# Routed experts in 71 tiles of 256 rows instead of 39 of 512

## The reference

```python
def _ffn(x, w1, w2, w3):
    return jax.nn.silu(x @ w1.T) * (x @ w3.T) @ w2.T
logits = xf @ router_w.T + expert_bias
rw, sel = jax.lax.top_k(logits, 2)
rw = jax.nn.softmax(rw)
combine = jnp.einsum('tk,tke->te', rw, jax.nn.one_hot(sel, 8))
# over the experts e: acc + combine[:, e, None] * _ffn(xf, w1[e], w2[e], w3[e])
```

## Time and profile before

| | us |
|---|---|
| median of three runs | 2825.15 |
| the profiled execution | 2823.8 |
| its span, on which all rows below lie | 2821.8 |
| the block of the routed experts, first row request to first request of the scan (789.61 to 1032.56) | 242.95 |

### The profile page before, as it was taken

One profiled execution on the slowest core, in us unless ns is written; L12 is line 12 of the kernel. 1 busy time (PEld: TensorE's weight loads), 2 busy tenths in 40 slices (PEclk: granted clock), 3 DMA queues, 4 the chain that ended last, 5 costly groups with the idle time before them and its releaser, 6 DMA issues. The chain is left out here.

```text
span 2821.8 us, 43246 instructions
## 1 busy us (share of the span) xinstructions
PE 2466.5 (87%) x13043; PEld 1468.7 (52%) x13058; DVE 2264.4 (80%) x3693; ACT 1704.3 (60%) x3383; POOL 2041.8 (72%) x1817
## 2 busy tenths in 40 slices
PE   7979999899979976989889898898999999995555
PEld 5646666566646642333333333333368888773222
DVE  5879999766634459999999999999867777777887
ACT  7847777743323235776667766676555555554665
POOL 5539999757746647999999999999546666664554
PEclk9979999999989987999999999999999999997555
DMA  5921111011145545545455454455523333320000
GB/s 170 422 60 22 23 23 23 7 33 44 42 130 165 153 124 183 189 172 197 171 186 186 175 193 172 186 185 203 182 83 91 88 86 88 87 81 19 19 19 23
DMA packets 238421, 331.80 MB, mean 118 GB/s; under 512 B 46433, under 2 KB 186998, under 8 KB 217346
## 3 DMA queue, kind: packets, MB, share of 16 engines
q1 hardware_dynamic: 227538, 311.48, 33.2%
q0 software_dynamic: 9088, 16.94, 1.7%
q10 hardware_dynamic: 1584, 0.79, 0.1%
HBM read 231.45 MB, written 99.50 MB: 117 GB/s over the span
## 5 line engine op out<-in xcount | busy, mean ns | idle before, releaser
L1870 POOL TENSOR_TENSOR s_drive<-s_du,s_b_sb 128x1024 f32<-128x1024 f32 x256 | 600.3, 2358 | 37.0 <-DVE s_state_ps L2237 36.8
L2237 DVE TENSOR_TENSOR_SCAN s_state_ps<-s_decay_ps,s_drive 128x512 f32<-128x512 f32 x416 | 487.1, 1216 | 42.8 <-ACT s_decay_ps L2023 33.5
L2385 PE MATMUL s_y_ps<-s_read,w_ident 128*128 128x512 f32 x832 | 406.7, 615 | 89.1 <-DVE s_read L2250 88.8
L2023 ACT ACTIVATE s_decay_ps<-s_delta,neg_rate 128x508 f32<-128x508 f32 x512 | 340.9, 682 | 152.0 <-DVE s_state_ps L2237 94.6
L2385 PEld LDWEIGHTS s_y_ps<-s_read,w_ident 128*128 128x128 f32 x832 | 149.3, 192 | 322.3 <-DVE s_read L2250 183.9
L2250 DVE TENSOR_TENSOR s_read<-s_state_ps,s_c_sb 128x1024 f32<-128x1024 f32 x208 | 254.7, 1224 | 7.2
L1416 POOL DMA_INDIRECT m_y_scratch<-e_y,e_index x156 | 152.5, 978 | 91.0 <-DVE e_y L1462 49.1
L2676 POOL TENSOR_TENSOR c_share<-c_p,c_norm 128x1232 f32<-128x1232 f32 x64 | 148.3, 2317 | 83.2 <-DVE c_norm L2809 83.2
L741 ACT ACTIVATE b_pT<-b_turn_ps 77x512 f32<-77x512 f32 x256 | 144.3, 591 | 74.6 <-PE b_turn_ps L873 74.6
L2879 PE MATMUL c_f_ps<-c_ctxT,w_c_wqk 128*128 128x308 f32 x512 | 178.4, 437 | 7.1 <-ACT c_k L2723 3.6
L1044 POOL DMA_INDIRECT m_rows_scratch<-m_xs,m_index x128 | 128.5, 1004 | 60.1 <-issue 39.9
(11 more groups left out here) (373 smaller groups left out, 6193.0 us busy)
## 6 DMA issues: line engine op xcount, KB each, us to landing
s_b_sb<-s_bc_scratch SPq DMA_DIRECT2D x64, 1024.0 KB, 6.2
s_c_sb<-s_bc_scratch SPq DMA_DIRECT2D x64, 1024.0 KB, 5.4
c_vp_scratch<-s_stage SPq DMA_DIRECT2D x152, 256.0 KB, 2.6
c_vp<-c_vp_scratch SPq DMA_DIRECT2D x64, 576.0 KB, 4.1
m_rows_scratch<-fill SPq DMA_DIRECT2D x33, 1040.0 KB, 27.0
e_w<-in_m_we_dram SPq DMA_DIRECT2D x39, 384.0 KB, 3.2
e_xg<-m_rows_scratch SPq DMA_DIRECT2D x39, 260.0 KB, 3.4
s_read<-m_y_scratch SPq DMA_DIRECT2D x32, 256.0 KB, 3.1
```

Source lines behind the costliest of these rows:

```text
L1870: nc.gpsimd.tensor_tensor(drive[:, (g * states + n) % drives, :, :], du[:, s, :, :], b_sb[:, n, :].unsqueeze(1).broadcast_to([128, halves, ...
L2023: nc.scalar.activation(decay[:, m, :, 1:], delta[:, s, m, :].rearrange("p (b t) -> p b t", t=T)[:, :, 1:], ACT.Exp, scale=core.neg_rate[:, ...
L2237: nc.vector.tensor_tensor_scan(home[:, h, :], decay[:, h, :, :].rearrange("p b t -> p (b t)"), drive[:, (g * states + n) % drives, h, :], ...
L2385: last = nc.tensor.matmul(y_ps[:, m, :], core.ident[:, :], read[:, r % deep, m, :], start=False, stop=False)
```

## The change

The tile of the routed experts gets a size of its own, `ET` = 256 rows; `TILES` becomes 2 * 8192 / 256 + 7 = 71. Both halves of the hidden units of a tile lie side by side in one PSUM bank (2 x 256 columns), so gate, value, result and transposed rows have two banks each, used in turn, and silu and the product run once for a tile, over 512 columns. PE's order becomes up(t), turn_x(t+2), down(t-1). SP first asks for the rows of four tiles, and then in turn for the weights of tile t and the rows of tile t+4. Rows and results have eight slots, weights five. The table is 71 entries wide.

```diff
+ET = 256
-LONGEST = B * T // GT
-TILES = 2 * B * T // GT + 7
+LONGEST = B * T // ET
+TILES = 2 * B * T // ET + 7
...
-    halves = 2
-    x_slots, w_slots, y_slots = 5, 3, 5
+    halves, lots = 2, ET // 128
+    x_slots, w_slots, y_slots, ahead = 8, 5, 8, 4
...
-        g_ps = ps("e_g_ps", [128, halves, GT])
-        u_ps = ps("e_u_ps", [128, halves, GT])
-        o_ps = ps("e_o_ps", [128, 2, GT])
-        turn_ps = ps("e_turn_ps", [128, GT])
+        g_ps = ps("e_g_ps", [128, 2, halves * ET])
+        u_ps = ps("e_u_ps", [128, 2, halves * ET])
+        o_ps = ps("e_o_ps", [128, 2, 512])
+        turn_ps = ps("e_turn_ps", [128, 2, 512])
...
-            for t in range(TILES):
+            def load_x(t):
                 first = sp.value_load(table[0][0:1, t:t + 1], min_val=0, max_val=8 * REGION)
-                owner = sp.value_load(table[1][0:1, t:t + 1], min_val=0, max_val=7)
                 if t >= x_slots:
                     sp.wait_ge(x_turned.sem, x_turned.at(t - x_slots, 1))
                     sp.wait_ge(y_ready.sem, y_ready.at(t - x_slots, 1))
                     sp.wait_ge(x_in[t % x_slots].sem, x_in[t % x_slots].at(t // x_slots, 0))
...
+            def load_w(t):
+                owner = sp.value_load(table[1][0:1, t:t + 1], min_val=0, max_val=7)
                 if t >= w_slots:
                     sp.wait_ge(downed.sem, downed.at(t - w_slots, 1))
...
+            for t in range(ahead):
+                load_x(t)
+            for t in range(TILES):
+                load_w(t)
+                if t + ahead < TILES:
+                    load_x(t + ahead)
...
             copy_xT(0)
+            copy_xT(1)
             for t in range(TILES):
-                if t + 1 < TILES:
-                    copy_xT(t + 1)
-                for n in range(halves):
-                    open_gate(t, n)
+                open_gate(t)
+                if t + 2 < TILES:
+                    copy_xT(t + 2)
...
-            def up(t, n):
+            def up(t):
                 pe.wait_ge(xT_ready.sem, xT_ready.at(t, 1))
                 landed(pe, w_in, t)
-                if t >= 1:
-                    pe.wait_ge(h_ready.sem, h_ready.at(t - 1, n + 1))
...
+                if t >= 2:
+                    pe.wait_ge(h_ready.sem, h_ready.at(t - 2, 1))
+                for n in range(halves):
+                    gate = nc.tensor.matmul(g_ps[:, t % 2, n * ET:(n + 1) * ET], w[:, t % w_slots, n, :],
+                                            xT[:, t % 2, :], start=True, stop=True)
+                gate.then_inc(g_ready.sem, 1)
+                for n in range(halves):
+                    value = nc.tensor.matmul(u_ps[:, t % 2, n * ET:(n + 1) * ET], w[:, t % w_slots, halves + n, :],
+                                             xT[:, t % 2, :], start=True, stop=True)
+                value.then_inc(u_ready.sem, 1)
...
             turn_x(0)
+            turn_x(1)
             for t in range(TILES):
-                if t + 1 < TILES:
-                    turn_x(t + 1)
-                up(t, 0)
+                up(t)
+                if t + 2 < TILES:
+                    turn_x(t + 2)
                 if t >= 1:
                     down(t - 1)
-                up(t, 1)
             down(TILES - 1)
```

More of the change, by code:

```diff
@@ L1242, in make_table @@
                 step(9)
-                nc.vector.tensor_scalar(table[0][:, :], start[:, :], float(routed * REGION // GT), float(GT),
+                nc.vector.tensor_scalar(table[0][:, :], start[:, :], float(routed * REGION // ET), float(ET),
                                         ALU.min, ALU.mult)
@@ L1351, in sig @@
             return core.sig(name, per_pass)
-        xg = sb("e_xg", [128, x_slots, GB, ROW])
+        xg = sb("e_xg", [128, x_slots, lots, ROW])
         w = sb("e_w", [128, w_slots, 3 * halves, 128])
[L1355 to L1359, removed]
-        g_ps = ps("e_g_ps", [128, halves, GT])
-        u_ps = ps("e_u_ps", [128, halves, GT])
-        o_ps = ps("e_o_ps", [128, 2, GT])
-        turn_ps = ps("e_turn_ps", [128, GT])
+        xT = sb("e_xT", [128, 2, ET])
+        silu = sb("e_silu", [128, 2, halves * ET])
+        h = sb("e_h", [128, 2, halves, ET])
+        y = sb("e_y", [128, y_slots, lots, D])
+        index = sb("e_index", [128, y_slots, lots], U32)
+        g_ps = ps("e_g_ps", [128, 2, halves * ET])
+        u_ps = ps("e_u_ps", [128, 2, halves * ET])
+        o_ps = ps("e_o_ps", [128, 2, 512])
+        turn_ps = ps("e_turn_ps", [128, 2, 512])
         x_in = [sig(f"e_x_in{n}", 16) for n in range(x_slots)]
@@ L1375, in run_experts @@
         y_ready = sig("e_y_ready")
-        scattered = [core.lasting(f"e_scattered{n}", 16 * GB) for n in range(y_slots)]
+        scattered = [core.lasting(f"e_scattered{n}", 16 * lots) for n in range(y_slots)]
         def landed(eng, slots, t):
@@ L1414, in _ @@
                 pool.wait_ge(y_ready.sem, y_ready.at(t, 1))
-                for j in range(GB):
+                for j in range(lots):
                     nc.gpsimd.indirect_dma_start(
@@ L1427, in copy_xT, with open_gate @@
                 if t >= 2:
[L1428 to L1432, removed]
-                if t >= 1:
-                    act.wait_ge(h_ready.sem, h_ready.at(t - 1, n + 1))
-                nc.scalar.activation(silu[:, n, :], g_ps[:, n, :], ACT.Silu).then_inc(silu_ready.sem, 1)
+                    act.wait_ge(u_ready.sem, u_ready.at(t - 2, 1))
+                nc.scalar.activation(xT[:, t % 2, :], turn_ps[:, t % 2, 0:ET], ACT.Copy).then_inc(xT_ready.sem, 1)
+            def open_gate(t):
+                act.wait_ge(g_ready.sem, g_ready.at(t, 1))
+                if t >= 2:
+                    act.wait_ge(h_ready.sem, h_ready.at(t - 2, 1))
+                nc.scalar.activation(silu[:, t % 2, :], g_ps[:, t % 2, :], ACT.Silu).then_inc(silu_ready.sem, 1)
             copy_xT(0)
+            copy_xT(1)
             for t in range(TILES):
-                if t + 1 < TILES:
-                    copy_xT(t + 1)
-                for n in range(halves):
-                    open_gate(t, n)
+                open_gate(t)
+                if t + 2 < TILES:
+                    copy_xT(t + 2)
         @block.vector
@@ L1450, in take_index, with hidden @@
                 nc.vector.tensor_copy(index[:, t % y_slots, :], xg[:, t % x_slots, :, D]).then_inc(indexed.sem, 1)
-            def hidden(t, n):
-                dve.wait_ge(silu_ready.sem, silu_ready.at(t, n + 1))
+            def hidden(t):
+                dve.wait_ge(silu_ready.sem, silu_ready.at(t, 1))
+                dve.wait_ge(u_ready.sem, u_ready.at(t, 1))
                 if t >= 2:
                     dve.wait_ge(downed.sem, downed.at(t - 2, 1))
-                nc.vector.tensor_tensor(h[:, t % 2, n, :], silu[:, n, :], u_ps[:, n, :],
-                                        ALU.mult).then_inc(h_ready.sem, 1)
+                nc.vector.tensor_tensor(h[:, t % 2, :, :].rearrange("p n c -> p (n c)"), silu[:, t % 2, :],
+                                        u_ps[:, t % 2, :], ALU.mult).then_inc(h_ready.sem, 1)
             def weigh(t):
                 dve.wait_ge(downed.sem, downed.at(t, 1))
-                for j in range(GB):
+                for j in range(lots):
                     last = nc.vector.tensor_scalar(y[:, t % y_slots, j, :], o_ps[:, t % 2, j * D:(j + 1) * D],
@@ L1467, in _ @@
                 take_index(t)
-                hidden(t, 0)
+                hidden(t)
                 if t >= 1:
                     weigh(t - 1)
-                hidden(t, 1)
             weigh(TILES - 1)
@@ L1477, in turn_x @@
                 landed(pe, x_in, t)
[L1478 to L1481, removed]
+                if t >= 2:
+                    pe.wait_ge(xT_ready.sem, xT_ready.at(t - 2, 1))
+                for j in range(lots):
+                    last = nc.tensor.transpose(turn_ps[:, t % 2, j * 128:(j + 1) * 128], xg[:, t % x_slots, j, 0:D],
                                                core.ident[:, :])
                 last.then_inc(x_turned.sem, 1)
-            def up(t, n):
+            def up(t):
                 pe.wait_ge(xT_ready.sem, xT_ready.at(t, 1))
                 landed(pe, w_in, t)
-                if t >= 1:
-                    pe.wait_ge(h_ready.sem, h_ready.at(t - 1, n + 1))
-                nc.tensor.matmul(g_ps[:, n, :], w[:, t % w_slots, n, :], xT[:, t % 2, :], start=True, stop=True)
-                nc.tensor.matmul(u_ps[:, n, :], w[:, t % w_slots, halves + n, :], xT[:, t % 2, :],
-                                 start=True, stop=True).then_inc(up_ready.sem, 1)
+                if t >= 2:
+                    pe.wait_ge(h_ready.sem, h_ready.at(t - 2, 1))
[7 more added lines that the diff above has]
+                value.then_inc(u_ready.sem, 1)
             def down(t):
-                pe.wait_ge(h_ready.sem, h_ready.at(t, halves))
+                pe.wait_ge(h_ready.sem, h_ready.at(t, 1))
                 if t >= 2:
```

(4 more changed lines are left out.)

13 lines of the change are left out of this document (7 added, 6 removed).

## The result

| kernel | median us | lowest to highest | ratio to before, 95% interval |
|---|---|---|---|
| before, beside the first runs of after | 2826.82 | 2822.27 to 2831.79 (6 runs) | |
| after | 2811.72 | 2806.02 to 2813.72 (6 runs) | 0.9944 [0.9934, 0.9954] |
| before, beside a second set of runs | 2828.74 | 2824.28 to 2834.55 (9 runs) | |
| after, second set (a1_again) | 2807.55 | 2803.28 to 2810.53 (5 runs) | 0.9924 [0.9910, 0.9938] |

The kernel is faster by 15.1 us in the first set, 0.56%, and by 21.2 us in the second, 0.76%. The forecast was 2803, some 22 us under the time before. Sign and mechanism came as forecast; the time lies 8.7 us above the forecast: inside the range of 2797 to 2815, but 1.7 us above the forecast's own range, which ended at 2810. The second set, at 2807.55, lies inside both.

What follows compares the result with a forecast made beforehand. PE's columns bound the block: columns -19.4, opening +0.6, close -1.4 and -1.4 sum to -21.6 us, from 2823.8 to 2802.2, said as 2803 since that execution is 1.35 under the median. Range 2797 to 2810, with rival (c) to 2815.

Steps and rivals of the forecast that it cites:

- Columns: PE in the experts' block: 18176 rows instead of 19968, 71 periods of 2.83 us instead of 39 of 5.66; -19.4 us.
- rival (c): PE: 256-column passes cost per column like 128-column ones, step switches some more; +4.5 to +9, 2808 to 2812, chance 0.12.
- the doubt: Whether half the rows take half PE's time: 256-column pass 0.215 us, or 0.223 at the 128's price, +4.5 us.
- Covers: Beside PE's 2.83 us: POOL 2.56, SP 2.28, DMA 78%, h 2.1 us early, weights 6.5 us to land; no price.
- rival (a): PE's up steps wait for late weights if landing exceeds 6.5 us; at 8 us 2838, slower; chance 0.05.
- Opening: Start of the block: four row requests precede the first weights, first up step at 796.3; +0.6, to +1.6 us.
- Half clock: PE at the block's opening: assumed at half clock for as long again as before; no difference.
- Close: End of the block: PE's idle 1.57 us falls to about 0.1, scatter tail 6.8 to some 5.4; -1.4 each.
- The 4 us allowed for scatter: Whole kernel: some 4 us of scatter between runs, counted into the forecast's own range of 2797 to 2810.

Runs made afterwards that it cites:

- c1_pool_more: The changed kernel with POOL also filling a spare tile of 512 columns before every tile's scatters; block 234.9 us.
- b4_et128: The changed kernel with 135 tiles of 128 rows instead of 71 of 256; block 336.7 us.
- d1_clear_last: The changed kernel with the clearing of spent semaphores and the two waits moved behind SP's last request; block 223.8 us.
- a3_warm: The changed kernel with five unread f32 dummy products on PE before and between the first transposes; block 223.0 us, total 2803.41 us.
- b1_slots512: The kernel before, keeping 39 tiles of 512 rows, with the new slots and request order; 2829.13 us, ratio 1.0002, block 246.8 us.
- a2_ahead0: The changed kernel with rows and weights requested in turn, no rows four tiles ahead; block 221.4 us, total 2808.57 us, ratio 0.9920.

## Why the prediction was right, and where its steps were off

**Columns: right.** This is the term that carried it, -19.4 of -21.6. The period is (997.34 - 809.84)/66 = 2.841 us, forecast 2.83. The pass of 256 columns that no row of before showed takes 0.865/4 = 0.216 us, forecast 0.215 with 0.223 as upper end; rival (c) falls. 71 x 0.011 = 0.8 us is all that the doubt was worth. The estimate by the Trainium skill's table (TensorE: Matmul & The Clock Gate, section Back-to-back issue gap), 0.218, is 1% over the measured pass. The Trainium skill's row on dims of 512 or more (TensorE: Matmul & The Clock Gate, section Why this matters for your kernels) is a target for the efficiency of a whole matmul, and prices no tile. In these rows passes of 256 columns cost 0.6% more a column than passes of 512 (0.845 ns for 0.840), which 9% fewer columns outweigh.

**Covers: right.** POOL, SP, h and the DMA share came as forecast: 2.56 of 2.84 us by c1_pool_more, 2.3 by b4_et128, no wait of PE, 0.79 for 78%. The weights landed in 3.4 to 4.4 us, median 3.8, where they took 3.2: against a cover of 6.5 us rival (a) had no chance, and it took the removal of two slots to see it. The rise of 0.6 us is in the sense of the Trainium skill (DMA: Bandwidth & Descriptors, section Latency and other measured facts), and a third of its 1.8; that load is the reason, no run shows.

**Opening: wrong by 1.8 us, above all because of a step that was not counted.** The sum let SP's first request come 0.66 us earlier, for a table read less. It came later: 2.2 us behind the release, 1.6 before. In the kernel before, `clear_spent` and the two waits stood behind the last request, beside other work; the change turns the loop body into functions and puts the loop below those lines, which the diff doesn't touch. d1_clear_last prices this at 1.2 us. With the lines moved back, SP's first request comes 1.0 us behind the release, 0.6 earlier than in before, as the sum had it, and the first up step 9.0 us behind it, 1.3 later than in before: that is the order, four row requests ahead of the first weights, taken at +0.6 with +1.6 as upper end.

**Half clock: wrong by 1.0 us.** "As long again" was an assumption. PE idled for 3.80 us before its first up step, and then ran 6.3 us at half clock (801.94 to about 808.2) where it had run 4.3 (795.71 to about 800.0). a3_warm, which fills the idle time, has none of it in its up steps. The length of the idle time alone doesn't settle it: b1_slots512 waited 2.78 us before its first up step and then ran some 3.0 us at half clock.

**Close: right in both terms, and one more.** The last two down steps stand in one line; it starts where the passes of 1003.66 end and takes 2.16 us where 16 passes take 1.95, so 0.2 us of idle time is left, forecast 0.1. POOL ends 5.2 us behind PE, forecast 5.4. Not foreseen were 1.2 us between POOL's end and the release, 1.1 of them POOL's drain. Without this term, which the sum had at nothing, the block would have missed by 3.4 us and not by 2.2.

**Total: 8.7 us over the forecast, of which 2.2 belong to the block.** The base is 1.7 (the kernel before had 2826.82 beside after, 2825.15 when the forecast was made), and 0.5 is the rounding of 2825.15 - 21.6 down to 2803. The other 4.3 lie outside the block: in the profiled executions cross attention 0 was 3.3 us longer and the scan 5.6, the quantised network 1.9 shorter. The profiled execution of the second set, 2803.28 us, shows the same program with a scan of 1007.4. The 4 us allowed for scatter were too few: the scan alone moves by 9. That 2811.72 is still inside the stated range is in part luck: it lies where rival (c) was to put it, 2808 to 2812, for whose sake the range ended at 2815 and not at 2810, and (c) did not come true. What was right is the block.

## What to carry to other kernels

When an engine is busy throughout and nobody keeps it waiting, count its columns first, and price everything else only as a cover that has to hold: here wider slots gained nothing, the new request order cost 3.5 us at the opening, and a smaller tile gained by halving the slack. Smaller tiles meet the fixed costs for a tile next, here two scatters at 2.56 us on POOL and two requests at 2.3 us on SP against 2.84 us of work, so the size can't be halved again. When a diff turns a loop into functions, list what the loop has moved past, unchanged lines too, and measure such a change by its block from release to release, not by the whole time.

## What the runs showed of the hardware

- PE's granted clock at an opening depends on what PE did just before. In after PE idled for 14.46 us before its first transposes and for 3.80 before its first up step, and stayed at 1.2 GHz (0.50) for 6.3 us of up steps. In a3_warm, with dummy products from the release at 788.0 on, it rose to 2.4 GHz by 793.3 and held through 2.69 us idle. The half-clocked part of the up steps was 4.3 us in before, 3.3 in a2_ahead0 and 3.0 in b1_slots512; what sets it stays open. In after, against a2_ahead0, the later start cost twice, by the wait (2.2 us) and by the clock behind it (1.5).
- POOL's drain at the end of the block depends on the program: 4.62 us in before, 3.48 in both executions of after and in all seven of its versions with 71 tiles, 5.60 in b1_slots512, 5.11 with 81 tiles, 2.41 with tiles of 128 rows. 1.1 us of the gain comes from there. What sets it no run here settles.
- Clearing the spent semaphores on SP takes 1.2 us, with the two waits behind it, when it stands ahead of a block's first request.
